# Graph kernel, counting of edges: four one-hot buffers, edge features squared inside PSUM, and one register load for two numbers of a node span

## What is computed

```
h = relu(layernorm(x));  x = x + L0(h)   # 10 hops: out = spmm(out) * 0.9 + h * 0.1
h = relu(layernorm(x));  x = x + L1(h)   # softmax aggregation per target
h = relu(layernorm(x));  x = x + L2(h)   # message MLP on [x[src], x[dst], edge_feat]
h = relu(layernorm(x));  x = x + L3(h)   # two graph convolutions
# inside L2:
def _mlp(h, W, b, gamma, beta):
    h = relu(h @ W + b)
    mu = mean(h, axis=0); var = mean(square(h - mu), axis=0)
    return gamma * (h - mu) * rsqrt(var + 1e-5) + beta
edge_feat = _mlp(edge_attr, W_edge, b_edge, g_edge, beta_edge)   # edge_attr: 100000 x 4
```

## Time and profile before

| | |
|---|---|
| median of 3 runs | 2900.73 us (2899.9 to 2903.26) |
| the profiled execution, its own time | 2895.72 us |
| its span | 2894.0 us |
| PE busy over the span | 1990.9 us (69%) |
| DVE busy | 1395.5 us (48%) |
| ACT busy | 780.0 us (27%) |
| POOL busy | 1011.5 us (35%) |

### The profile page before, as it was taken

One profiled execution on the slowest core, in us unless ns is written; L12 is line 12 of the kernel. 1 busy time (PEld: TensorE's weight loads), 2 busy tenths in 40 slices (PEclk: granted clock), 3 DMA queues, 4 the chain that ended last, 5 costly groups with the idle time before them and its releaser, 6 DMA issues. The chain is left out here.

```text
span 2894.0 us, 51972 instructions
## 1 busy us (share of the span) xinstructions
PE 1990.9 (69%) x15441; PEld 1606.3 (56%) x15442; DVE 1395.5 (48%) x2559; ACT 780.0 (27%) x1318; POOL 1011.5 (35%) x1142
## 2 busy tenths in 40 slices
PE   1777677778999999678546565646556555655489
PEld 0333344458999999545345455535445454554477
DVE  7857766655444444555534343424334333433642
ACT  1686466541111111111212122212212221222110
POOL 3211221122000000000076776766767667664000
PEclk9989998778999999889756565655656655556789
DMA  4211111110000000700122222222222222222100
GB/s 140 83 49 37 54 53 53 67 61 1 2 2 2 2 2 23 280 1 4 35 51 52 46 50 49 49 48 47 50 48 49 49 49 46 49 48 31 58 2 17
DMA packets 86636, 132.96 MB, mean 46 GB/s; under 512 B 48616, under 2 KB 55656, under 8 KB 86462
## 3 DMA queue, kind: packets, MB, share of 16 engines
q1 hardware_dynamic: 59214, 88.38, 9.5%
q0 software_dynamic: 25344, 38.98, 6.7%
q10 hardware_dynamic: 1904, 3.21, 0.4%
HBM read 95.89 MB, written 34.58 MB: 45 GB/s over the span
## 5 line engine op out<-in xcount | busy, mean ns | idle before, releaser
L1341 POOL DMA_INDIRECT counts<-p_rows,rows x784 | 836.8, 1067 | 353.7 <-issue 258.4
L1510 PE MATMUL ps_e_z<-e_w_q,counts 128*128 128x96 f32 x1584 | 316.4, 383 | 348.2 <-ACT counts L1468 225.1
L929 PE MATMUL ps_hop<-y,counts 128*128 128x192 f16 x6250 | 525.7, 247 | 24.6 <-DVEq L816 12.1
L929 PEld LDWEIGHTS ps_hop<-y,counts 128*128 128x128 f16 x6250 | 520.2, 98 | 30.0 <-DVEq L816 12.1
L1510 PEld LDWEIGHTS ps_e_z<-e_w_q,counts 128*128 128x128 f32 x1584 | 302.5, 293 | 378.5 <-ACT counts L1468 236.4
L1521 PE MATMUL ps_e_seg<-counts 128*128 128x96 f32 x1584 | 314.1, 363 | 164.7 <-issue 133.9
L1521 PEld LDWEIGHTS ps_e_seg<-counts 128*128 128x128 f32 x1584 | 285.6, 270 | 215.6 <-issue 213.0
L559 DVE TENSOR_TENSOR hot_w<-iota_w,places_now 128x1600 f16<-128x1600 f16 x300 | 297.2, 991 | 181.2 <-PE ps_counts L585 169.8
L585 PE MATMUL ps_counts<-hot_w,hot_p 128*128 x1196 | 294.9, 379 | 128.7 <-DVE hot_p L559 80.3
L1468 ACT ACTIVATE counts<-ps_e_u 96x1024 f32<-96x1024 f32 x99 | 101.0, 1020 | 825.8 <-remote 542.2
L526 POOL TENSOR_TENSOR places_now<-places,origins (+1 forms) x302 | 116.9, 387 | 452.2 <-DVE hot_p L559 280.5
(11 more groups left out here) (343 smaller groups left out, 2161.7 us busy)
## 6 DMA issues: line engine op xcount, KB each, us to landing
counts<-count_rows SPq DMA_DIRECT2D x30, 800.0 KB, 6.8
count_rows<-attr_split SPq DMA_DIRECT2D x25, 800.0 KB, 3.8
counts<-p_rows,rows POOLq DMA_INDIRECT x784
e_attr<-attr_parts SPq DMA_DIRECT2D x99, 72.0 KB
attr_parts<-attr_split SPq DMA_DIRECT2D x9, 784.0 KB, 16.3
attr<-attr_parts SPq DMA_DIRECT2D x50, 140.6 KB
e_dst_rows<-dst_row SPq DMA_DIRECT2D x99, 64.0 KB
e_w_q<-q_rows SPq DMA_DIRECT2D x396, 12.0 KB
```

The source lines that it names most:

```text
L929: mm = pe.matmul(ps[:, r, 0:2 * D], k.counts[:, m, b, :], y[:, odd, b, :], start=b == 0, stop=b == NB - 1)
L1341: nc.gpsimd.indirect_dma_start(z[:, slot, j, :], None, k.p_rows, bass.IndirectOffsetOnAxis(rows, 0)) \
L1510: mm = pe.matmul(ps_z[:, two, j // (STEP_TILES // 2), at:at + D], u_hot[:, two, j * P:(j + 1) * P], w_q[:, fed, j // Q_TILES, :], start=Tr ...
```

## The change

Four edits. `hot_p` and `hot_w` get four buffers each in place of two; `hot_used` starts at 4. Relu and Square of the edge features write their elements into `ps_u`, where they come from, and the SBUF tile `u` is gone; PE therefore waits for the Square of the unit before (`u_summed`) and no longer for its Relu (`u_taken`) when it wants `ps_u` again. ACT's Relu no longer waits for the Square before it. `window_tabs` holds the two numbers of a window side by side, and POOL loads both registers with one instruction.

```diff
+    HOTS = 4
-        hot_p = sb("hot_p", [P, 2, BATCH, P], F16)
-        hot_w = sb("hot_w", [P, 2, BATCH, WIDE], F16)
+        hot_p = sb("hot_p", [P, HOTS, BATCH, P], F16)
+        hot_w = sb("hot_w", [P, HOTS, BATCH, WIDE], F16)
-        u = sb("u", [D, U_PARTS, U_EDGES], F32)
...
+        def last_and_shift(w):
+
+            _, pair = nc.values_load_multi_w_load_instructions(
+                k.window_tabs[0:1, bass.ds(w + 1, 1), :].rearrange("p a c -> p (a c)"), [mybir.EngineType.Pool])
+            return pair
...
-                    last = last_of(pool, w)
-                    shift = pool.value_load(k.window_tabs[0:1, bass.ds(w + (1 + NW), 1)])
+                    last, shift = last_and_shift(w)
...
-                    s = q % 2
+                    s = q % HOTS
...
-            pe.sem_inc(hot_used, 2)
+            pe.sem_inc(hot_used, HOTS)
...
-                    pe.wait_ge(u_taken, n)
+                    pe.wait_ge(u_summed, n)
...
             def rectified(n):
                 act.wait_ge(u_done, n + 1)
-                if not isinstance(n, int) or n:
-                    act.wait_ge(u_summed, n)
-                nc.scalar.activation(u[:, :, :], ps_u[:, :, 0:U_EDGES], ACT.Relu,
+                nc.scalar.activation(ps_u[:, :, 0:U_EDGES], ps_u[:, :, 0:U_EDGES], ACT.Relu,
                                      accum_out=u_sums[:, 0, bass.ds(n, 1)]).then_inc(u_taken, 1)
 
             def squares(n):
                 act.wait_ge(u_taken, n + 1)
-                nc.scalar.activation(u[:, :, :], u[:, :, :], ACT.Square,
+                nc.scalar.activation(ps_u[:, :, 0:U_EDGES], ps_u[:, :, 0:U_EDGES], ACT.Square,
                                      accum_out=u_sums[:, 1, bass.ds(n, 1)]).then_inc(u_summed, 1)
```

More of the change, by code:

```diff
@@ L123, in program @@
         with ExitStack() as part:
-            k.window_tabs = part.enter_context(nc.sbuf_tensor("window_tabs", [1, 1 + 2 * NW], I32))
+            k.window_tabs = part.enter_context(nc.sbuf_tensor("window_tabs", [1, NW + 1, 2], I32))
             k.places = part.enter_context(nc.sbuf_tensor("places", [P, TILES + BATCH, 2], F32))
@@ L373, in _ @@
             dve.wait_ge(row_made, 1)
-            nc.vector.memset(k.window_tabs[:, 0:1], -1)
-            step(nc.vector.tensor_copy(k.window_tabs[:, 1:1 + 2 * NW], ps_row[:, 0:2 * NW]))
+            nc.vector.memset(k.window_tabs[:, 0, :], -1)
+            step(nc.vector.tensor_copy(k.window_tabs[:, 1:1 + NW, :],
+                                       ps_row[:, 0:2 * NW].rearrange("p (c n) -> p n c", c=2)))
             dve.wait_ge(based, 2)
@@ L453, in last_of @@
         def last_of(eng, w):
-            return eng.value_load(k.window_tabs[0:1, bass.ds(w + 1, 1)])
+            return eng.value_load(k.window_tabs[0:1, bass.ds(w + 1, 1), 0])
+        def last_and_shift(w):
+            _, pair = nc.values_load_multi_w_load_instructions(
+                k.window_tabs[0:1, bass.ds(w + 1, 1), :].rearrange("p a c -> p (a c)"), [mybir.EngineType.Pool])
+            return pair
         def units_of(d):
@@ L585, in window @@
                         mm = pe.matmul(ps[:, j % 2, 0:WIDE],
-                                       hot_p[:, bass.ds(i & 1, 1), t, :].rearrange("p a s -> p (a s)"),
-                                       hot_w[:, bass.ds(i & 1, 1), t, :].rearrange("p a s -> p (a s)"),
+                                       hot_p[:, bass.ds(i & (HOTS - 1), 1), t, :].rearrange("p a s -> p (a s)"),
+                                       hot_w[:, bass.ds(i & (HOTS - 1), 1), t, :].rearrange("p a s -> p (a s)"),
                                        start=False, stop=False, skip_group_check=True)
```

## The result

| | before | after |
|---|---|---|
| median | 2900.32 us (2896.29 to 2903.26, 4 runs) | 2925.15 us (2918.38 to 2926.07, 4 runs) |
| ratio after / before | | 1.0066, interval 1.0044 to 1.0089 |
| profiled execution, its span | 2895.72, 2894.0 | 2924.76, 2923.0 |
| mean granted clock | 0.774 | 0.764 |

The change makes the kernel slower. The ratio times the median of before is 2900.32 x 1.0066 = 2919.5 (2913 to 2926); the median of the four runs, 2925.15, lies 4 us above the upper end of the range (2921). The direction was forecast, the size was too small: +10 was said, and the ratio gives +19, the two medians +25 and the two profiled executions +29. With 2919.5 the time is above the forecast's own 2905 to 2918 and just inside the whole range, which goes to 2921.

The account below looks back on a forecast made before the run. Bounds taken: DVE's one-hots in block 0, ACT's own work in blocks 1 to 4, PE's issuing later. 10.3 + 3.9 - 0.8 - 3.0 - 0.3 = +10.1 us, 2911 on the 2900.73 median; own range 2905 to 2918, whole range 2899 to 2921.

Parts of the forecast that it names:

- The step of the early chain: Blocks 0 to 4: Relu-to-Relu step grows from 4.56 to 5.05 us; over 21 steps +10.3 us.
- The clock term: Blocks 2 to 4: feature matmuls 0.88 us longer at half clock, a third of the time, over 13 steps: +3.9 us.
- my rival of the further fall: PE's clock falls further in blocks 1 to 4; all 21 steps at half give 18.5 us, time 2926; chance 0.12 for over 2918.
- a few us either way: Late blocks: the phase of PE's slow pieces against the blocks may shift, a few us either way; not in the sum.
- Four buffers, -3.0,: Block 0: a deeper one-hot queue gives back half of DVE's 6.0 us wait for a free buffer, -3.0 us.
- Late blocks: From block 5 on PE's issuing sets the pace and one-hots are ready early, so four buffers gain nothing there.
- The first rival: Faster: PE truly waits for one-hots in late blocks; four buffers remove over 16 of 33.0 us; chance 0.08.
- Writing to PSUM, -0.8,: ACT in the early chain: source and destination in PSUM save 0.04 us a unit over 21 steps, -0.8 us.
- the no-change rival: Each activation of a step loses 0.17 us on PSUM, so the new step is 4.71; time 2895 to 2906.5, chance 0.22.
- One load, -0.3,: POOL, start of the stage: DVE's 8.0 us wait there gets one load shorter, -0.3 us; nothing elsewhere.

Follow-up runs that it names:

- e4: The kernel before with one word changed: PE waits for the Square, not the Relu, of the unit before; SBUF tile u, two buffers, two loads stay. Ratio 1.0068.
- e2: The kernel before with Relu and Square written to PSUM and PE waiting for the Square; two buffers, two loads. Ratio 1.0061.
- e8: The changed kernel with early feature units spread over blocks 0 to 8, from block 1 on one in every second window. Ratio 0.997 to the kernel before.
- e5: The changed kernel with five matmuls of zeros ahead of the feature matmuls in blocks 1 to 4, not at a block's first unit. Ratio 1.002 to the kernel before.
- b1: The kernel before, unchanged, profiled once more on another chip: 2893.76 us.
- e1: The changed kernel with hot_p and hot_w in two buffers again. Ratio 1.0067 to the kernel before.
- b2: The kernel before, unchanged, profiled once more on another chip: 2705.79 us.

## Why the prediction was right in direction and too small

In short: the mechanism was the one forecast, the closed chain of PE and ACT, and e4, e2 and e8 show it. The clock's term was less than half of what it came to, the gain from four buffers did not come, and some 9 us had no term. All of these went the same way.

**The step of the early chain** was right: 5.05 said, 5.08 measured at the full clock, 5.93 at half (5.9 said). At 5.08, 21 steps cost 21 x (5.08 - 4.56) = 10.9 against 10.3 said. That the wait alone does it is shown by e4, where one word costs 0.68%. PE's start behind the read-out was 0.14 and not 0.1.

**The clock term is the one that was mis-sized.** Its step was "a third of the time runs at the half level": 13 steps x 0.34 x 0.88 = 3.9. I took the share of slow time from the kernel before. I also counted it for the 13 steps of blocks 2 to 4 alone. The new wait lengthens the pauses of PE, and in blocks 2 to 4 the granted clock fell from 0.83 to 0.68, in block 1 from 0.95 to 0.81; ten steps were long, and two in part: 10 x 0.85 + 0.5 + 0.4 = 9.4. e5 bears the mechanism out, since work in the pauses takes 8.0 back. The page "TensorE: Matmul & The Clock Gate" of the Trainium skill (What's actually happening) has the clock fall after idle time; by that rule my rival of the further fall should have had more than 0.12. The rival itself, all 21 steps at half, didn't come about either: 9.4 lies between 3.9 and 18.5. Still, the time lies above 2918, where I had put only that 0.12. Which steps become long, no row of before told; with the Square in PSUM it was ten or eleven of 21 in four executions, with the wait alone five.

**Block ends, the late blocks and the messages** had no term. Blocks 1 to 4 grew by 21.5, of which the chains within them are 18.9; the remaining 2.6 lie between the chains. From the last Relu of block 3 to the first of block 4 it is 15.92 in place of 14.32, at a granted clock of 0.71 in place of 0.79, and one block earlier 12.21 in place of 11.41, at 0.90 in place of 1.00; that the clock makes them is argued from these two pairs. Blocks 10 to 24 added 3.5, since blocks 10 and 12 took 18.2 and 18.1 in place of 16.0 and 16.5: they joined the pattern of 16.0 and 18.05 sooner. The prediction said "a few us either way" of this phase, and the unchanged kernel has it too: b1 alternates from block 10 on, as after does, and its blocks 10 to 24 take 256.8 against 256.6. The messages added 3.2 with the same matmuls, and why stays open.

**Four buffers, -3.0,** was wrong: +1.0 in block 0 with the two longer steps in it (+1.5), that is -0.5, and DVE's waiting for PE there went from 6.0 to 6.5. I had asked which engine is slow at each moment and not what is late next: PE reached the first unit sooner and waited 4.05 for its transfer, where it had waited 0.45. Two buffers in the changed kernel (e1) cost nothing that the ratios show.

**Late blocks.** "In the late blocks PE does not wait for one-hots" held. With four buffers the idle time put down to DVE is 36.5 where it was 33.0, in as many pieces, in the same stretch (after, 389 to 651.3):

```profile
PE ps_counts L591 <- DVE hot_p L565: 36.5, 23, 2.2
```

The first rival needed it to fall by 16. The blocks 5 to 9 changed by 0.3. Doubling the queue in front of PE took nothing from this idle time. And DVE is not behind: in the same stretch it waits 95.8 us for PE to free a buffer, in 91 pieces. So the name of DVE there is an attribution and no wait for its work.

**Writing to PSUM, -0.8,** was right in sign and somewhat too small: 21 x 0.06 = -1.3, and the no-change rival (0.17 an activation) is refuted by 1818 and 1823 ns, 0.01 and 0.05 less. **One load, -0.3,** is not seen: DVE's wait for POOL at the start is 8.05 where it was 7.95. The stage does start 0.7 earlier, at 57.73, but its start moves by itself: 58.09 to 58.82 in the executions with two loads, 57.26 to 59.23 in those with one. That the edit alone is 0.2 to 0.35% faster had no term, and its place was not found.

The sum by its own steps, with what was measured: 10.9 + 9.4 + 2.6 + 3.5 + 3.2 - 0.5 - 0.7, and +0.5 of the graph convolutions, +0.2 of the hops and -0.3 of blocks 5 to 9, is 28.8 on the profiled execution (29.0 measured; the cheaper Square is in the 5.08, and the -0.5 holds block 0's rest). Over runs the ratio gives 19, so part of the 29 belongs to this pair of executions. Against b1, whose late blocks have the same pattern, blocks 1 to 24 of after are 19.5 longer (526.3 against 506.8), where they are 24.8 longer than in the first profile of before.

## What to carry to other kernels

Before a wait is moved to a later event of the same engine, write down the closed chain that it makes (here feature matmuls, Relu, Square, and round again) and compare it with the step of today; saved SBUF or some hundredths of a microsecond an activation do not pay for two engines that take turns, but spacing the work so that they need not (e8) does. Where a change adds pauses to PE, take the granted clock of the stretch as something that falls with them, and give the term the range from today's share to all steps at half. Doubling a buffer gains only up to what is late next, and idle time "put down to" a producer is tested by looking whether the producer's row had ended, and by comparing the same stretch once the queue is deeper.

## What the runs showed of the hardware

- PE with 0.76 of its time busy in blocks 2 to 4 was granted 0.68 of full speed (after, 88.97 of 116.90), with 0.77 busy 0.87 (e5, 83.67 of 108.80), and before, also with 0.76 busy, 0.83. The busy share of a stretch doesn't tell its clock; added work without use made the stretch shorter.
- The same program runs its late blocks either in 16.0 and 18.05 us by turns or in 16.2 on average. In the kernel before, blocks 10 to 24 take 242.8 (b2) or 256.8 (b1). Both patterns appear also in kernels with the Square in PSUM (after 16.0 and 18.05, e2 16.2).
- The stage of messages took about 1198 us on one chip and 1012 on another with the same kernel (before and b2); an indirect DMA on POOL took 1067 ns on the first and 978 on the second. That stage on the two chips, and POOL's group on the second:

```profile
1453.00:2651.00 1198.00, 689.45 (x3334) 596.69 (x3334) 465.09 (x591) 260.77 (x294) 831.67 (x781) 0.61 0.22 48
```

```profile
1448.00:2460.50 1012.50, 653.10 (x3334) 593.34 (x3334) 464.32 (x591) 254.43 (x294) 761.24 (x781) 0.66 0.25 57
```

```profile
L1341 POOL DMA_INDIRECT counts<-p_rows,rows x784 | 766.5, 978 | 238.9 <-issue 238.9
```

- ACT writes its elements to PSUM as fast as to SBUF or slightly faster (1818 against 1829 ns for 96x2000), and one load of two registers costs 520 ns, nearly two of 287.
